# Routing stage of a vision kernel: one scale on the dispatch weights in place of two norms, one of two rows normalised on GpSimd, ring of ten

## What is computed

```python
h  = _layernorm(h + attention(h))             # (x - m) / sqrt(v + eps)
xn = _rms_norm(h, norm_weight, 1e-5)          # h * rsqrt(mean(h*h) + eps) * weight
tok = _l2_normalize(xn)
sl = _l2_normalize(slots) * scale[:, None]    # 64 slots
logits = einsum('sd,btd->bst', sl, tok)
dispatch_w = softmax(logits, axis=-1)         # over tokens
combine_w = softmax(logits, axis=-2)          # over slots
y = einsum('btd,bst->bsd', xn, dispatch_w)
```

## Time and profile before

| | us |
|---|---|
| median of 3 runs (4807.69 to 4813.0) | 4812.62 |
| profiled execution | 4837.32 |
| its span, first to last instruction | 4835.4 |
| busy over the span: PE, PEld | 4495.4, 3885.2 |
| busy over the span: DVE, ACT, POOL | 3048.0, 2720.1, 2701.4 |
| routing pass, first load issue to last stores, about | 3760 to 4290 |

### The profile page before, as it was taken

How to read it: one execution, slowest core, us unless ns; L and a number is a source line. 1 busy time by engine, 2 the same in 40 slices (tenths; PEclk the granted TensorE clock), 3 DMA queues, 4 the chain that set the end, 5 groups by cost and what they waited for, 6 DMA issues and landing times. The chain is left out here.

```text
span 4835.4 us, 161306 instructions
## 1 busy us (share of the span) xinstructions
PE 4495.4 (93%) x48311; PEld 3885.2 (80%) x48311; DVE 3048.0 (63%) x8728; ACT 2720.1 (56%) x6788; POOL 2701.4 (56%) x4491
## 2 busy tenths in 40 slices
PE   8999999899999999999979999999999788889965
PEld 8999999688888888888868888888887566678853
DVE  4555555566666666666647777777776799930058
ACT  3444444466666666666635555555555477753346
POOL 3444444466666666666646666666666588841135
PEclk9999999899999999999979999999999799999965
DMA  6777777677777777777756666666664233369978
GB/s 170 202 202 202 203 202 201 151 166 165 168 168 167 168 166 168 165 165 167 169 110 141 145 142 145 142 146 143 146 141 111 76 93 93 93 156 247 241 233 258
DMA packets 697918, 789.88 MB, mean 163 GB/s; under 512 B 367345, under 2 KB 519887, under 8 KB 697840
## 3 DMA queue, kind: packets, MB, share of 16 engines
q1 hardware_dynamic: 697840, 788.92, 67.6%
HBM read 519.30 MB, written 265.72 MB: 162 GB/s over the span
## 5 line engine op out<-in xcount | busy, mean ns | idle before, releaser
L770 DVE TENSOR_REDUCE a_mx<-a_sq 99x2 f32<-99x394 f32 x1536 | 797.3, 560 | 378.5 <-PE a_sq L821 378.2
L770 DVE TENSOR_REDUCE c_mx<-c_sq 99x2 f32<-99x198 f32 (+1 forms) x1536 | 641.8, 458 | 255.9 <-PE c_sq L821 254.6
L713 ACT ACTIVATE a_ex<-a_sk 99x792 f32<-99x792 f32 (+1 forms) x768 | 638.1, 831 | 107.8 <-PE a_sk L843 57.3
L713 ACT ACTIVATE c_ex<-c_sk 99x792 f32<-99x792 f32 (+1 forms) x768 | 509.4, 663 | 208.2 <-PE c_sk L837 137.7
L379 PE MATMUL e_tokp<-e_wmap,e_ptT 128*99 128x192 f32 x3072 | 544.2, 327 | 20.8 <-DVE e_cvar L332 20.8
L379 PEld LDWEIGHTS e_tokp<-e_wmap,e_ptT 128*99 128x99 f32 x3072 | 483.2, 167 | 21.2 <-issue 20.8
L821 PE MATMUL a_sq<-a_ks,a_qs 96*99 96x198 bf16 x3072 | 441.1, 255 | 31.6 <-DMA a_ks<-scr_qk 16.6
L634 POOL TENSOR_SCALAR_AFFINE_SELECT c_ex<-c_ex 99x396 f32<-99x396 f32 (+1 forms) x768 | 408.0, 546 | 91.5 <-ACT c_ex L713 82.0
L282 POOL CAST e_parts<-e_rest 96x396 bf16<-96x396 f32 x256 | 176.4, 689 | 482.5 <-DVE e_rest L338 482.5
L821 PE MATMUL c_sq<-c_ks,c_qs 96*99 96x99 bf16 (+1 forms) x3072 | 424.8, 231 | 0.0
L843 PE MATMUL a_sk<-a_qs,a_ks 99*99 99x198 bf16 (+1 forms) x3072 | 408.7, 254 | 2.7 <-issue 2.1
(11 more groups left out here) (196 smaller groups left out, 11575.7 us busy)
## 6 DMA issues: line engine op xcount, KB each, us to landing
e_ptT<-in_x SPq DMA_DIRECT2D x128, 594.0 KB
x_w<-in_fc SPq DMA_DIRECT2D x128, 576.0 KB, 6.6
scr_qk<-e_parts SPq DMA_DIRECT2D x128, 445.5 KB
scr_qk<-a_parts SPq DMA_DIRECT2D x128, 445.5 KB
scr_tv<-e_tv SPq DMA_DIRECT2D x128, 288.0 KB
a_tv<-scr_tv SPq DMA_DIRECT2D x128, 288.0 KB
scr_tv<-a_res SPq DMA_DIRECT2D x128, 288.0 KB
c_tv<-scr_tv SPq DMA_DIRECT2D x128, 288.0 KB
```

Of the source, the lines that this page charges most:

```text
L713: nc.scalar.activation(to, of, ACT.Exp).then_inc(exped.sem, 1)
L770: nc.vector.reduce_max(mx[:, b2.parity, qt, h:h + 2], sq[f % 2][:, :, 0:width], AX.X).then_inc(maxed.sem, 1)
```

## The change

The RMS norm and the layer norm of a token become one factor. `r_xn` is now the centred token times the weight, without either scale; the factor XS, to the power -0.5 of XIN = var (1+eps) + eps², comes in later, as a scale on the dispatch weights `r_dT`, which ScalarE copies with two scaled instructions where there was one copy. The powers RSTD and XS are one GpSimd instruction on four elements. The RMS power, RIN and INV are gone. The guard compares with XIN times a constant. Row 1 of `r_h2` is written by GpSimd, row 0 by VectorE. R is 10.

```diff
-    R = 8
+    R = 10
...
             def step(c):
                 if c.inside(n):
                     sp.wait_ge(normed.sem, normed.at(c - R))
+                    sp.wait_ge(normed0.sem, normed0.at(c - R))
+                    sp.wait_ge(scaled.sem, scaled.at(c - R))
...
                 if b1.inside(n):
                     pool.wait_ge(var_eps.sem, var_eps.at(b1))
-                    pool.tensor_tensor(st[:, b1.place, RSTD], st[:, b1.place, VAR], half[:], ALU.pow).then_inc(rstd.sem, 1)
-                if b3.inside(n):
-                    pool.wait_ge(ms_eps.sem, ms_eps.at(b3))
-                    pool.tensor_tensor(st[:, b3.place, RMS], st[:, b3.place, RIN], half[:], ALU.pow).then_inc(rms.sem, 1)
+                    pool.wait_ge(w_copied.sem, w_copied.at(b1 - R))
+                    pool.tensor_tensor(st[:, b1.place, RSTD:XS + 1], st[:, b1.place, VAR:XIN + 1], half[:],
+                                       ALU.pow).then_inc(rstd.sem, 1)
+                if b2.inside(n):
+                    pool.wait_ge(rstd.sem, rstd.at(b2))
+                    pool.wait_ge(h_stored.of(b2 - R), h_stored.at(b2 - R))
+                    m.hold(pool)
+                    pool.tensor_scalar(h2[:, b2.place, 1], hp[:, b2.place, 1], mv[:, b2.place, 1, 0:1],
+                                       st[:, b2.place, RSTD, 1:2], ALU.subtract, ALU.mult).then_inc(normed.sem, 1)
...
-                    nc.scalar.copy(dT[:, b9.parity], dTp[:]).then_inc(w_copied.sem, 1)
+                    for t in range(2):
+                        nc.scalar.mul(dT[:, b9.parity, t], dTp[:, t], st[:, b9.place, XS, t:t + 1]).then_inc(w_copied.sem, 1)
...
-                    for t in range(2):
-                        nc.vector.tensor_scalar(h2[:, p, t], hp[:, p, t], mv[:, p, t, 0:1], st[:, p, RSTD, t:t + 1],
-                                                ALU.subtract, ALU.mult).then_inc(normed.sem, 1)
+                    nc.vector.tensor_scalar(h2[:, p, 0], hp[:, p, 0], mv[:, p, 0, 0:1], st[:, p, RSTD, 0:1],
+                                            ALU.subtract, ALU.mult).then_inc(normed0.sem, 1)
...
-                    dve.wait_ge(rms.sem, rms.at(b4))
+                    dve.wait_ge(y_done.sem, y_done.at(b4 - R))
                     for t in range(2):
-                        nc.vector.scalar_tensor_tensor(out=xn[:, p, t], in0=h2[:, p, t], scalar=st[:, p, RMS, t:t + 1],
-                                                       in1=normw[:], op0=ALU.mult, op1=ALU.mult).then_inc(scaled.sem, 1)
+                        nc.vector.scalar_tensor_tensor(out=xn[:, p, t], in0=hp[:, p, t], scalar=mv[:, p, t, 0:1],
+                                                       in1=normw[:], op0=ALU.subtract, op1=ALU.mult).then_inc(scaled.sem, 1)
...
-                if b2.inside(n):
-                    p = b2.place
-                    dve.wait_ge(inv_var.sem, inv_var.at(b2))
-                    for t in range(2):
-                        nc.vector.tensor_scalar(st[:, p, RIN, t:t + 1], st[:, p, INV, t:t + 1], mv[:, p, t, 1:2], LN_EPS,
-                                                ALU.mult, ALU.add).then_inc(ms_eps.sem, 1)
...
-                    nc.vector.tensor_scalar(st[:, b5.place, NIN], st[:, b5.place, NN], 1e-10, None, ALU.max).then_inc(guarded.sem, 1)
+                    nc.vector.scalar_tensor_tensor(out=st[:, b5.place, NIN], in0=st[:, b5.place, XIN], scalar=GUARD,
+                                                   in1=st[:, b5.place, NN], op0=ALU.mult, op1=ALU.max).then_inc(guarded.sem, 1)
...
-                    dve.wait_ge(var_eps.sem, var_eps.at(b1))
-                    nc.vector.reciprocal(st[:, b1.place, INV], st[:, b1.place, VAR]).then_inc(inv_var.sem, 1)
+                    nc.vector.tensor_scalar(st[:, b1.place, XIN], mv[:, b1.place, :, 1], 1.0 + LN_EPS, LN_EPS * LN_EPS,
+                                            ALU.mult, ALU.add).then_inc(var_eps.sem, 1)
```

More of the change, by code:

```diff
@@ L992, in route_pass @@
         slotsT = m.sb("r_slotsT", [CH, 2, SLOTS])
-        half = m.sb("r_half", [TT, 2])
+        half = m.sb("r_half", [TT, 2, 2])
         hp = m.sb("r_hp", [TT, R, 2, D])
@@ L1008, in route_pass @@
         fill = m.sb("r_fill", [128, 640], BF16)
-        VAR, RSTD, INV, RIN, RMS, NN, NIN, RN, NMAX, DEN, RDEN = range(11)
+        VAR, XIN, RSTD, XS, NN, NIN, RN, NMAX, DEN, RDEN = range(10)
+        GUARD = 1e-10
         xtp = m.ps("r_xtp", [CH, 2, SP])
@@ L1024, in route_pass @@
         mean_var = m.event("r_mean_var", 2)
-        var_eps = m.event("r_var_eps")
+        var_eps = m.event("r_var_eps", 2)
         rstd = m.event("r_rstd")
[L1027 to L1030, removed]
+        normed0 = m.event("r_normed0")
+        normed = m.event("r_normed")
         scaled = m.event("r_scaled", 2)
@@ L1045, in route_pass @@
         w_turned = m.event("r_w_turned", 2)
-        w_copied = m.event("r_w_copied", 2)
+        w_copied = m.event("r_w_copied", 3)
         y_done = m.event("r_y_done")
@@ L1067, in step @@
                     sp.wait_ge(normed.sem, normed.at(b))
+                    sp.wait_ge(normed0.sem, normed0.at(b))
                     sp.dma_start(scr["h2"][b.number], h2[:, b.place]).then_inc(h_stored.of(b), 16)
@@ L1080, in _ @@
         def _(pool):
-            for e in (rstd, rms, rnorm, combine, dispatch):
+            for e in (rstd, normed, rnorm, combine, dispatch):
                 e.seed(pool)
             pool.wait_ge(prep, 5)
-            pool.tensor_tensor(scale[:, 2:3], scale[:, 1:2], half[0:SLOTS, 0:1], ALU.pow).then_inc(prep_pow, 1)
+            pool.tensor_tensor(scale[:, 2:3], scale[:, 1:2], half[0:SLOTS, 0, 0:1], ALU.pow).then_inc(prep_pow, 1)
             pool.wait_ge(prep_pow, 1)
             def step(c):
-                b1, b3, b5, b8 = c - 1, c - 3, c - 5, c - 8
+                b1, b2, b5, b8 = c - 1, c - 2, c - 5, c - 8
                 if b8.inside(n):
@@ L1099, in step @@
                     pool.wait_ge(var_eps.sem, var_eps.at(b1))
-                    pool.tensor_tensor(st[:, b1.place, RSTD], st[:, b1.place, VAR], half[:], ALU.pow).then_inc(rstd.sem, 1)
-                if b3.inside(n):
-                    pool.wait_ge(ms_eps.sem, ms_eps.at(b3))
-                    pool.tensor_tensor(st[:, b3.place, RMS], st[:, b3.place, RIN], half[:], ALU.pow).then_inc(rms.sem, 1)
+                    pool.wait_ge(w_copied.sem, w_copied.at(b1 - R))
[7 more added lines that the diff above has]
+                                       st[:, b2.place, RSTD, 1:2], ALU.subtract, ALU.mult).then_inc(normed.sem, 1)
                 if b5.inside(n):
                     pool.wait_ge(guarded.sem, guarded.at(b5))
-                    pool.tensor_tensor(st[:, b5.place, RN], st[:, b5.place, NIN], half[:], ALU.pow).then_inc(rnorm.sem, 1)
+                    pool.tensor_tensor(st[:, b5.place, RN], st[:, b5.place, NIN], half[:, 0], ALU.pow).then_inc(rnorm.sem, 1)
             pipeline(pool, n, DEPTH, R, step)
@@ L1146, in _ @@
         def _(dve):
-            for e in (stats, mean_var, var_eps, inv_var, normed, ms_eps, scaled, guarded, logits, maxed, recip):
+            for e in (stats, mean_var, var_eps, normed0, scaled, guarded, logits, maxed, recip):
                 e.seed(dve)
```

## The result

The change makes the kernel slower: 4829.49 us (median of six runs, 4823.85 to 4833.81) against 4808.76 for the kernel before (six runs); the ratio is 1.0044, 95% interval 1.0031 to 1.0057, so +20.7 us where +23.4 was forecast. The profiled execution of after took 4829.66 us, its span is 4828.0.

The account below looks back on a forecast made before the run. The prediction took the VectorE-GpSimd ring, 3.79 us a step, to bound the routing pass. Its terms gave a step of 4.027, 0.203 more over 116 steps, so 23.4 us on 4812.62: 4836, range 4805 to 4890.

Parts of the forecast that it names:

- GpSimd's own list: GpSimd's instructions of one routing step end to end: about 3.3 us before, 3.68 after the change without a single wait.
- guard held by `r_dw`: VectorE's guard, with two SBUF inputs, waits 0.345 us beside GpSimd's `r_dw`, delaying VAR, XIN and the power; `r_h` at 4.00.
- ring 1: VectorE from `r_h` to VAR, GpSimd's RSTD power, next `r_h`: sets the step at 3.79 us, undisturbed 3.72 after.
- The power on four elements: GpSimd's RSTD power, widened to four elements, takes 1.017 us as in the last pass, against 0.71 before.
- The row-1 pass: GpSimd's new pass over row 1 of `r_h2`, two operations on 192 elements: 0.85 us taken, 0.77 to 1.36 kept.
- The RN power beside `r_xn`: GpSimd's RN power reads while VectorE's `r_xn` runs and is delayed by 0.15 us, with ends 0 and 0.33.
- the prediction's two signs that the hold is wrong: In the changed kernel's trace: a guard of 0.2 us and a step below 3.85 us.
- The rival "the guard is not held": The guard reads only two elements, so the power starts with `r_dw`'s end: `r_h` at 3.77, 4809 us; chance 0.21.
- TensorE's ring as the floor: TensorE with VectorE, transpose of the logits to the next: needs 3.73 us a step, so no step gets shorter.
- The turns of the loop: Each turn of the hardware loop adds time, 0.027 us a step on the step of 4.00.
- The rival of the clock: TensorE's clock falls because a longer step leaves it more idle; at worst part of +186 us; chance 0.03.

Follow-up runs that it names:

- e1: Changed kernel with both rows of `r_h2` back on VectorE, the power on four elements kept on GpSimd; 5047.93 us, ratio 1.0502, with the clock falling to 0.50.
- e8: Changed kernel with the power on two elements, row 1 still on GpSimd, the dispatch weights' own scale left out; 4795.37 us, ratio 0.9963.
- e5: Changed kernel with the second operation of GpSimd's row-1 pass left out, so row 1 is only centred; 4836.93 us, ratio 1.0056.
- e3: Changed kernel with the guard as a maximum with a constant, one tensor input; 4825.72 us in the one run of four without the clock fall.
- e2: Changed kernel with both `r_h2` rows on VectorE and the power split into two of two elements, the second two images later; 4799.21 us, ratio 0.9986.
- e9: Changed kernel with a ring of eight tiles in place of ten; 4827.71 us, ratio 1.004.
- e4: Changed kernel with GpSimd's row-1 pass placed behind the RN power; 5087.24 us, ratio 1.0576, with the clock falling to 0.50.
- e6: Kernel before with a ring of ten and nothing else; 5074.71 us, ratio 1.0574, with the clock falling to 0.50.

## Why the prediction was right, and where it was wrong

The sign, the size and the place are as forecast: a step of 4.007 for a forecast of 4.027, on the two engines named, with GpSimd without idle time. The path is not the one forecast: GpSimd's own list sets the step, and not a guard held by `r_dw`. Step by step:

- **The bound before**: ring 1 at 3.79. The runs agree; e1 shows that a longer power on this ring is paid in the step.
- **The power on four elements**: 1.017 reckoned from another pass, 1.016 measured. e8 shows that it alone decides the sign.
- **The row-1 pass**: 0.85 taken, 1.011 measured, inside the bounds of 0.77 to 1.36. One operation is 0.768, just the lower end; the second costs 0.24, neither nothing nor as much as the first. The term was 0.16 too small.
- **The RN power beside `r_xn`**: +0.15 estimated, +0.17 measured (0.865 against 0.69). It starts 0.19 into `r_xn`; in before it starts 0.24 ahead of `r_xn` and is not stretched, and in e5, 0.02 behind its start, it takes 0.72.
- **The guard held by `r_dw` for 0.345**: wrong, and this was the step on which the forecast stood. The guard takes 0.17 to 0.22 inside `r_dw`, and e3 without its second input gives the same step. Of the prediction's two signs that the hold is wrong, a guard of 0.2 and a step below 3.85, only the first came. The rival "the guard is not held" was right in its mechanism: the power starts with the end of `r_dw`. It gave 3.77 and 4809 because its list was too short by 0.23.
- **A hold that was not foreseen**: `r_h` on VectorE, which has one tensor input in SBUF, takes 0.57 beside the row-1 pass and 0.38 alone (e1). It lifts ring 1 from the 3.72 reckoned to 3.91, and inside the loop the 0.19 from XIN to the power, where 0.09 was reckoned, lifts it to 4.00. e5 shows this ring at 4.03 with GpSimd no longer full.
- **TensorE's ring as the floor**: put at 3.73, with "more than this cannot be won"; e8's steps of 3.69 are under it.
- **The turns of the loop**: 0.027 a step was kept. No step inside after's loop is longer than 4.01: at a turn `r_h` starts 0.14 after the power's end instead of 0.04, but takes 0.47 instead of 0.57, so the turn costs nothing.

So the sum came out by luck, because two errors of the same size met. The hold of the guard lifted the forecast from the list's 3.77 to 4.00, by 0.23; and the list is itself 4.00, 0.23 more than reckoned: the pass 0.15 (0.98 from its start to RN's, for 0.83), the start of the pass 0.04 later against `r_h`, the RN power 0.03, the rest 0.01. What the change gives, three of 18 instructions a step off VectorE and a power of 0.76 off GpSimd, went into one place: the power between XIN and `r_h`, which stands on ring 1 and in GpSimd's full list at once. That is why relieving GpSimd's list alone (e1, e5) gives nothing, and shortening the power (e8), or splitting it where GpSimd has room (e2), gives all. Ahead of the loop GpSimd's list leads in after (4.01 against 3.91 for ring 1, by e5's rows); inside it the two lie at the same height.

The rival of the clock had 0.03 and did not come in after's six runs; but the edge is near. e3, whose steps are those of after, fell in three runs of four, while e9, of the same step, fell in none of twelve, and before, with 3.79, fell in two of 82. So a longer step alone does not decide it. In e3 the fall of the profiled run came after a wait of TensorE of 0.91 for the logits, where the step before had 0.74. At 0.50 a step takes 6.1 for the rest of the pass, and it cost some 245 us (5070 less 4825.72), more than the +186 that the prediction gave as the worst; the prediction reckoned a step there at 5.4. What decides whether it falls is open.

## What to carry to other kernels

A small operation on the path between two engines can be dear by its elements: two further elements of a power cost 0.31 us in every step here, more than the `r_h` instruction that VectorE was spared (0.295). Before an operation is merged with one that stands on a ring, ask whether its result is wanted at that point of the ring; if not, give it a place of its own where the engine idles. When two limits lie at the same height, an experiment that relieves one shows little; look for the one operation that is on both. A sum that comes out is no proof of its path: the line of the one instruction on which it stands, here the guard, has to be read too.

## What was not expected of the hardware

- GpSimd's pass over 192 elements holds VectorE's scalar instruction with one SBUF input (0.38 to 0.57), while the guard, a two-input instruction on two elements, is not held beside `r_dw` (0.17 to 0.22) and is beside `r_cw` (0.39, e4). The Trainium skill, page "SBUF — State Buffer", section "Who interferes with whom", names as able to contend with GpSimd both instructions with two SBUF inputs and `tensor_scalar`, which can enter a mode that uses two ports. The held `r_h` is a `tensor_scalar` and agrees with that, though no run shows in which mode it ran; the guard beside `r_dw` does not agree. The prediction had only the first of the two.
- Beside `r_dw`, VAR of two elements takes 0.16 when it starts 0.35 after `r_dw` and 0.33, ending with it, when it starts 0.48 after it (after and e5). In before, 0.66 after it, VAR takes 0.16 again. So the hold depends on when in GpSimd's instruction the other one comes, not on its whole length.
- With ten places in before's ring VectorE stood 3.1 and 1.5 us at its first turn of the loop with nothing to wait for, and the clock that fell behind it did not come back in that pass (e6).
- The same power starts 0.10 after XIN in the written-out steps of e1 and e5 and 0.19 after it inside their loops, with GpSimd idle both times. In e5's loop the trace has a register operation of GpSimd's at this place in each step (L1103, 43 ns), which the written-out steps do not have; how much of the 0.09 is its doing no run separates.
